# A three-part network over eight images: the first expert layer over sorted (token, expert) blocks, written out without a loop

## What is computed

```python
def _L0(x):                      # on the group-normalised image, 8 experts, hidden 384
    logits = x @ Wg + bg
    _, top_idx = top_k(logits, 2)
    gates = softmax(where(chosen, logits, -inf))
    y = gelu(x @ W1[e] + b1[e]) @ W2[e] + b2[e]          # for every expert e
    return sum_e y[e] * gates[e]
x = x + _L0(gn(x))               # 32 groups of 3 channels over all tokens
t = tokens(x)
t = t + causal_attention(ln(t))  # 6 heads of 16
t = t + _L1_ffn(ln(t))           # 4 experts, top 2 of softmax, hidden 384
```

## Time and profile before

| what | value |
|---|---|
| median of 3 runs | 1535.62 us (1528.77 to 1542.92) |
| profiled execution, span | 1533.6 us |
| instructions | 36404 |
| PE matmul busy | 1324.4 us, 86% |
| ACT busy | 934.1 us, 61% |
| DVE busy | 893.8 us, 58% |
| POOL busy | 716.0 us, 47% |
| DMA moved | 35.14 MB |

### The profile page before, as it was taken

How to read it: one execution, slowest core, us unless ns; L and a number is a source line. 1 busy time by engine, 2 the same in 40 slices (tenths; PEclk the granted TensorE clock), 3 DMA queues, 4 the chain that set the end, 5 groups by cost and what they waited for, 6 DMA issues and landing times.

```text
span 1533.6 us, 36404 instructions
## 1 busy us (share of the span) xinstructions
PE 1324.4 (86%) x12957; PEld 775.0 (51%) x12957; DVE 893.8 (58%) x2662; ACT 934.1 (61%) x1880; POOL 716.0 (47%) x656
## 2 busy tenths in 40 slices
PE   4778879888898899889898899888998898968978
PEld 1554543565536564466635565365644665333445
DVE  4865593388617784287724886177832866165362
ACT  2566537566675667656675667656676666703755
POOL 4765540467406572367605573075713665000355
PEclk9897998999999999899998999899999999956989
DMA  5000200300021000400004000210003000120100
GB/s 108 12 1 18 46 1 12 75 2 2 12 54 32 2 2 23 71 7 2 2 22 76 1 2 16 52 32 2 2 23 65 1 2 2 38 48 1 23 12 11
DMA packets 37424, 35.14 MB, mean 23 GB/s; under 512 B 26091, under 2 KB 28012, under 8 KB 37234
## 3 DMA queue, kind: packets, MB, share of 16 engines
q1 hardware_dynamic: 20594, 26.37, 8.8%
q10 hardware_dynamic: 16640, 6.29, 1.9%
HBM read 22.62 MB, written 9.63 MB: 21 GB/s over the span
## 4 chain that ended last, share of the span: by engine, by line
PE 30%; issue 26%; POOL 21%; DVE 13%; DMA 4%; ACT 2%; DVEq 1%; POOLq 1%; SPq 1%; ACTq 0%
POOL hidl L628 20%; PE ps_y L647 11%; PE ps_u L647 9%; PE ps_r L647 6%; DVE mpart L1156 4%; PE ps_m L647 3%; DVE xn L1138 1%; DMA ks<-qk_dram 1%; DMA qk_dram<-qk_l 1%; DVE acc L1104 1%; ACT hidh L934 1%; DVE yt L1288 1%; POOLq L608 1%; PE ps_m L666 1%; POOL rstd L609 1%
## 5 line engine op out<-in xcount | busy, mean ns | idle before, releaser
L628 POOL TENSOR_TENSOR hidl<-hid,hidh 128x512 f16<-128x512 f32 x576 | 670.7, 1185 | 686.2 <-ACT hidh L934 684.1
L933 ACT ACTIVATE hid<-ps_u 128x512 f32<-128x512 f32 x576 | 345.0, 599 | 391.8 <-PE ps_u L647 363.2
L1156 DVE TENSOR_REDUCE mpart<-ps_r 128x1 f32<-128x512 f32 (+2 forms) x576 | 297.3, 549 | 94.1 <-PE ps_r L647 79.8
L934 ACT ACTIVATE hidh<-ps_u 128x512 f16<-128x512 f32 x576 | 344.4, 598 | 0.0
L647 PEld LDWEIGHTS ps_y<-w2s,hidh 128*128 128x128 f16 x4608 | 276.4, 101 | 119.2 <-issue 24.1
L647 PE MATMUL ps_y<-w2s,hidh 128*128 128x96 f16 x4608 | 326.3, 210 | 8.0 <-DVE acc L1104 7.2
L647 PE MATMUL ps_r<-ks,qs 96*128 96x512 f16 (+2 forms) x576 | 199.9, 363 | 66.9 <-DVE mpart L1156 39.4
L647 PE MATMUL ps_y<-w2s,hidl 128*128 128x96 f16 x2304 | 231.0, 211 | 26.7 <-POOL hidl L628 26.6
L647 PE MATMUL ps_u<-xah,w1h 97*128 97x512 f16 x408 | 168.7, 414 | 29.8 <-ACT hidh L934 12.8
L965 ACT ACTIVATE probs<-ps_r 128x512 f32<-128x512 f32 (+3 forms) x352 | 152.9, 506 | 57.6 <-PE ps_r L647 57.2
L647 PE MATMUL ps_u<-xah,w1l 97*128 97x512 f16 x408 | 168.1, 412 | 0.0
(11 more groups left out here) (188 smaller groups left out, 1582.0 us busy)
## 6 DMA issues: line engine op xcount, KB each, us to landing
rb<-rsum_dram SPq DMA_DIRECT2D x24, 256.0 KB, 4.2
qs<-qk_dram SPq DMA_DIRECT2D x24, 192.0 KB, 4.9
ks<-qk_dram SPq DMA_DIRECT2D x24, 192.0 KB, 4.8
xin<-in_x_dram ACTq DMA_DIRECT2D x8, 384.0 KB, 4.1
qk_dram<-qk_h SPq DMA_DIRECT2D x16, 192.0 KB, 3.1
qk_dram<-qk_l SPq DMA_DIRECT2D x16, 192.0 KB, 3.5
out_dram<-xo ACTq DMA_DIRECT2D x8, 384.0 KB, 3.0
w_raw<-in_L_conv_W_dram SPq DMA_DIRECT2D x8, 288.0 KB, 5.1
```

The source lines that it names most:

```text
L628: g.tensor_tensor(hidl[:, grp.k % 2, j, :], hid[:, j, :], hidh[:, grp.k % 2, j, :], ALU.subtract).then_inc(hl_ready, 1)
L933: a.activation(hid[:, j, :], bank[:], ACT.Gelu, scale=1.0 / WS)
L934: a.activation(hidh[:, grp.k % 2, j, :], bank[:], ACT.Gelu, scale=1.0 / WS).then_inc(h_ready, 1)
L1156: v.tensor_reduce(mpart[:, h, i, part:part + 1], ps_r[k % 3][:, 0:w], AX, ALU.max).then_inc(mx_free, 1)
```

## The change

The first expert layer is computed only for the chosen pairs. Each image has 2048 (token, expert) pairs. They are sorted by expert, each expert's list is filled up to whole blocks of 128, and 23 blocks, a number fixed at build time, hold every possible split. The sorted order is made on the chip. DVE finds the two experts of each token; PE counts the earlier pairs of each expert by matmuls with a triangle of ones (`rank`); DVE turns counts into row numbers `slots` and the expert of each block `expert_of`. POOL scatters the rows of the image `xtok` into `xs_dram`, 16 indirect DMAs of 128 rows (`scatter`), SP loads all of it back (`xs_load`), and PE turns it and ACT and DVE split it (`xs_turn`, six quads: five of 4 blocks, one of 3).

The weights of a block's expert come by a DMA whose source is read from `expert_of` into a register of SP (`fetch`), 344 KB each, into a ring of 16 slots, `wring`. The first 16 blocks of an image are fetched in stage C before it (`prefetch`), the other seven when a quad is done (`refill`). The split weights are written to DRAM (`wq_dram`) once, at the start. A quad takes the place of a group: `first_layer` makes nine matmuls of 128 columns for each block in place of 512 columns for one expert, and the second layer has one matmul more a tile, which adds the bias. ACT copies the result out (`y_take`), SP stores it (`y_dram`), and POOL gathers it in token order, another 16 indirect DMAs (`gather`). DVE multiplies by the gates and adds (`merge`). Matmuls for the biases by the gates go away in both layers.

The stages are A, S, C in place of A, C, S, and C holds the q, k and value projections, 26 of the 72 maxima, the sums of the softmax and the sorting in of the next image; A holds the other 46 maxima; S holds routing, gather, merge, ln1 and scatter. `maxima` stands in slot 25 of the 28 of stage A, right before S. Image 1's iteration has its own table, with all 72 in slots 20 to 27 of stage A. The loop over images is written out: every iteration from -1 to 10 is unrolled. Image loads and stores move from ACT's queue to SP's. Layer normalisation is applied by two operations over half an image in place of one a tile.

```diff
+NBLK = (TOP * T + EA * (P - 1)) // P
+QUADS = [range(n, min(n + TC, NBLK)) for n in range(0, NBLK, TC)]
+GA, GC = len(QUADS), NC * EC
...
+def steps(it):
+
+
+    for n in range(GA + 1):
+        up = group_a(it, n) if n < GA else None
+        down = group_a(it, n - 1) if n else group_c(it - 3, GC - 1)
+        for j in range(TC):
+            yield Step("a", TC * n + j, up, down, j)
+    for n in range(STEPS + 2):
+        yield Step("s", n, None, None, n)
+    for n in range(GC):
+        up = group_c(it - 2, n)
+        down = group_c(it - 2, n - 1) if n else None
+        for j in range(TC):
+            yield Step("c", TC * n + j, up, down, j)
...
+NORM = [(15, "x_turn", 0, 1), (17, "x_turn", 1, 1), (18, "gn_stats", 0, 1), (20, "gn_mean", 0, 1),
+        (22, "gn_spread", 0, 1), (24, "gn_apply", 0, 1), (26, "logits_a", 0, 1), (27, "route_a", 0, 1)]
+ROUTE = [(0, "route_a", 1, 1), (0, "route_a", 2, 1), (2, "rank", 0, 1), (2, "exp_a", 0, 1)]
+IN_A = [(4, "store", 0, -3), (8, "x_load", 0, 1), (1, "ln2", 0, -2), (3, "ln2", 1, -2),
+        (5, "ln2_apply", 0, -2), (6, "ln2_apply", 1, -2), (9, "x2_turn", 0, -2), (11, "x2_turn", 1, -2),
+        (13, "logits_c", 0, -2), *maxima_at(0, 24, MAX_C, MAXU, -1), (25, "maxima", 0, -1), *NORM]
+IN_S = [(0, "exp_c", 0, -2), *ROUTE, (2, "gather", 0, 0), (2, "gather", 1, 0),
+        (5, "route_c", 0, -2), (6, "route_c", 1, -2), (7, "route_c", 2, -2), (8, "route_c", 3, -2),
+        (10, "merge", 0, 0), (11, "ln1", 0, 0), (11, "scatter", 0, 1), (11, "scatter", 1, 1), (13, "ln1_apply", 0, 0),
+        (16, "merge", 1, 0), (16, "gate_a", 0, 1), (17, "ln1", 1, 0), (17, "scatter", 2, 1), (17, "scatter", 3, 1),
+        (19, "ln1_apply", 1, 0), (21, "x1_turn", 0, 0), (24, "x1_turn", 1, 0)]
+IN_C = [(0, "sums", 0, -1), (1, "qk", 0, 0), (2, "xs_load", 0, 1), (3, "qk", 1, 0), (5, "qk", 2, 0), (7, "qk", 3, 0),
+        (8, "sum_inverse", 0, -1), (9, "val", 0, 0), (11, "val", 1, 0),
+        *maxima_at(15, TC * GC - 1, 0, MAX_C, 0), *fetches(range(12, 28, 2)),
+        (14, "normalise_y", 0, -1), (15, "normalise_y", 1, -1),
+        *sorted_in(range(13, 31, 3), 1), (27, "project", 0, -1), (30, "project", 1, -1)]
...
+            def fetch(b, blk):
+                s, _ = ring(b, blk)
+                e = sp.value_load(expert_of[0:1, b % 2, blk:blk + 1], min_val=0, max_val=EA - 1)
+                sp.dma_start(wring[:, s, :], wq_dram[bass.ds(e, 1)].rearrange("a p f -> p (a f)")
+                             ).then_inc(w_in[s], 16)
+
+            routed_end = 0
+
+            def prefetch(b, k):
+                if k == 0:
+                    sp.wait_ge(slots_ready, b + 1)
+                    if b:
+                        sp.wait_ge(y_full, routed_end)
+                for blk in range(2 * k, 2 * k + 2):
+                    fetch(b, blk)
+
+            def refill(group):
+
+                for blk in QUADS[group.n]:
+                    if blk + RING < NBLK:
+                        if blk == QUADS[group.n][0]:
+                            sp.wait_ge(y_full, grp.k)
+                        fetch(group.b, blk + RING)
...
+                if name == "xs_load":
+                    sp.wait_ge(scattered, 16 * TOP * TT * (b + 1))
+                    wait(sp, xs_ready, GA * b)
+                    if b > 1:
+                        sp.wait_ge(merged, NC * b)
+                    sp.dma_start(xs[:], xs_dram[b % 2].rearrange("(b q) c -> q b c", q=P)).then_inc(xs_in, 16)
...
+                if name == "gather":
+                    if k == 0:
+                        for i in range(YBUFS):
+                            pool.wait_ge(y_out[i], 16 * (GA // YBUFS) * (b + 1))
+                        pool.wait_ge(xs_ready, GA * max(b + 1, 2))
+                    for t in range(TC * k, TC * (k + 1)):
+                        for n in range(TOP):
+                            g.indirect_dma_start(
+                                out=ygot[:, n, t, :], out_offset=None, in_=y_dram[b % 2],
+                                in_offset=bass.IndirectOffsetOnAxis(ap=slots[:, b % 2, n, t:t + 1], axis=0)
+                            ).then_inc(gathered[k], 16)
+                if name == "scatter":
+                    if k == 0:
+                        pool.wait_ge(slots_ready, b + 1)
+                        pool.wait_ge(x_loaded, 16 * (b + 1))
+                        wait(pool, xs_in, 16 * (b - 1))
+                        if b < 2:
+                            pool.wait_ge(xs_zeroed, 32)
+                    for t in range(2 * k, 2 * k + 2):
+                        for n in range(TOP):
+                            g.indirect_dma_start(
+                                out=xs_dram[b % 2],
+                                out_offset=bass.IndirectOffsetOnAxis(ap=slots[:, b % 2, n, t:t + 1], axis=0),
+                                in_=xtok[:, b % XBUFS, t, :], in_offset=None).then_inc(scattered, 16)
...
+            def rank(b):
+
+                pe.wait_ge(mask_ready, b + 1)
+                shared()
+                mm(ps_m[:, 0:EA * (TT + 1)], before[:], maskb[:].rearrange("p t e -> p (t e)"), True, False)
+                for t in range(TT):
+                    last = mm(ps_m[:, EA * (t + 1):EA * (TT + 1)].rearrange("p (t e) -> p t e", e=EA), onesb[:],
+                              maskb[:, t:t + 1, :].to_broadcast([P, TT - t, EA]), False, t == TT - 1)
+                last.then_inc(m_full, 1)
+
...
+                    for i, blk in enumerate(QUADS[group.n]):
+                        s, use = ring(group.b, blk)
+                        if j == 0:
+                            pe.wait_ge(w_in[s], 16 * (use + 1))
+                        slot = slice(P * blk, P * (blk + 1))
+                        last = split(bank[:, P * i:P * (i + 1)], wring[0:ONE + 1, s, P * j:P * (j + 1)],
+                                     wring[0:ONE + 1, s, HID + P * j:HID + P * (j + 1)],
+                                     xsh[:, slot], xsl[:, slot], True)
...
+                mm(out, select[:], b2, True, False)
...
+            def y_take(group, seq):
+
+                k = group.b * GA + group.n
+                w = D * len(QUADS[group.n])
+                act.wait_ge(y_full, seq + 1)
+                wait(act, y_out[k % YBUFS], 16 * (k // YBUFS))
+                a.activation(ysort[:, k % YBUFS, :, :].rearrange("p b d -> p (b d)")[:, 0:w],
+                             ps_y[seq % 2][:, 0:w], ACT.Copy)
+                act.drain().then_inc(y_sorted, 1)
+                act.nop().then_inc(y_free[0], 1)
...
+                    blks = QUADS[k]
+                    w = P * len(blks)
+                    wait(act, xs_ready, GA * b + k - 1)
+                    shared()
+                    a.activation(xsf[:, k % 2, 0:w], ps_m[0:D, 0:w], ACT.Identity, bias=gshift[:], scale=grstd[:]
+                                 ).then_inc(xsf_ready, 1)
+                    a.activation(xsh[0:D, P * blks[0]:P * blks[0] + w], ps_m[0:D, 0:w], ACT.Identity,
+                                 bias=gshift[:], scale=grstd[:]).then_inc(m_free, 1)
...
+                if name == "merge":
+                    dve.wait_ge(gathered[k], 16 * PER_HALF * (b + 1))
+                    for n in range(TOP):
+                        v.tensor_tensor(ygot[:, n, tiles, :], ygot[:, n, tiles, :],
+                                        gate_a[:, n, tiles].unsqueeze(2).to_broadcast([P, TC, D]), ALU.mult)
+                    dve.drain()
+                    v.tensor_tensor(ygot[:, 0, tiles, :], ygot[:, 0, tiles, :], ygot[:, 1, tiles, :], ALU.add)
+                    dve.drain()
+                    v.tensor_tensor(xb[:, tiles, :], xb[:, tiles, :], ygot[:, 0, tiles, :], ALU.add
+                                    ).then_inc(merged, 1)
```

More of the change, by code:

```diff
@@ new lines, in maxima_at, with sorted_in, fetches @@
+def maxima_at(first, last, n0, n1, off):
+    return [(slot, "max", n0 + k, off) for slot, ks in spread(n1 - n0, range(first, last + 1)).items() for k in ks]
+MAX_C = 26
+def sorted_in(slots, off):
+    return [(slot, "xs_turn", q, off) for q, slot in enumerate(slots)]
+def fetches(slots):
+    return [(slot, "prefetch", n, 1) for n, slot in enumerate(slots)]
+NORM = [(15, "x_turn", 0, 1), (17, "x_turn", 1, 1), (18, "gn_stats", 0, 1), (20, "gn_mean", 0, 1),
+        (22, "gn_spread", 0, 1), (24, "gn_apply", 0, 1), (26, "logits_a", 0, 1), (27, "route_a", 0, 1)]
@@ L278, in run_chores, with chores @@
+def chores(table, it, step):
+    for name, unit, off in table[step.phase].get(step.slot, ()):
+        if off is None:
+            yield name, unit, 0
+        elif 0 <= it + off < NIMG:
+            yield name, unit, it + off
 def run_chores(m, chore, some):
@@ L521, in stack_qk @@
+                wait(sp, qk_out, 64 * b + 32 * (s + 1))
                 dst, parts = ((qs, (0, 1, 0)), (ks, (0, 0, 1)))[s]
@@ new lines, in _ @@
+            for it in range(-1, LAST_IT + 1):
+                table = schedule(it)
+                for s in steps(it):
```

(40 more changed lines are left out.)

1387 lines of the change are left out of this document (673 added, 714 removed).

## The result

The changed kernel takes 1608.4 us (median of 4 runs, 1607.9 to 1612.6) against 1536.5 for the kernel before, measured beside it: a ratio of 1.047, 95% interval 1.043 to 1.051. It is slower by 4.7%, where 1370 us was forecast. The profiled execution's span is 1610.8 us.

A forecast was written before the change was run, and what follows sets the result against it. No engine was full on average: PE and POOL together paced A and C, PE and ACT bound S. Start 293, six periods of 148 (888) and tail 187 gave 1368 us, so 1370; range 1240 to 1500.

The forecast's parts named there:

- Part 3: Stage S after the change: a chain on POOL of gathers, rstd and scatters sets its length, taken as 43 us.
- c: POOL's time for one indirect DMA of 128 rows, taken as 1.2 us; no row of the profile showed it.
- 13 + 24c: Length of S: 4 + 16c for gathers, 2, 8c for scatters, 2 and 5; 42 us, taken as 43.
- a rival at 15 in 100: In S, DVE and POOL shut each other out during descriptor writing: +15 us in S, 1470 us; 15 in 100.
- overhang: After S, C's first group waits for POOL's last scatters, about 8c less 5; taken as 5 us.
- The one rival that had the kernel slower than before, at 9 in 100: POOL's indirect DMAs in S and at the start decide: c = 2.3 gives 1635 us; 9 in 100.
- Part 5: Stage C after the change: PE 43 us, ACT 41, DVE 35, SP's queue level with the stage; taken as 50 (45 to 58).
- SP's queue decides: Rival: SP's queue or late weights (3 us a fetch) make PE wait for w_in; 1460 us, 8 in 100.
- Part 6: Outside the period: prologue 75 to 80 us, image 2's start at 293, six periods 888, tail 187; sum 1368 us.
- Parts 1, 2 and 4: PE's expert work 21.7 us for 55.5; stage A 43 us; maxima chain before S charged 4 + 3 us an image.

The follow-up runs named there:

- both faults out: Changed kernel with plain gathers and scatters on SP's queue, q and k first in C, sorted rows loaded at the end of S: 1403.7 us.
- v1: Against the version with gathers one a slot and scatters in C: scatters one at a time, eight in S and eight in C: 1512.7 us.

## Why the prediction was wrong

The forecast was 1368 us for the span, and it came to 1611: 104 us more at the start, 155 in the six full periods (1043 for 888; five near 179 and the last 150), 16 less in the tail (171 for 187).

**Part 3, stage S: the step that failed.** c was right: 1.25 from gather to gather for 1.2. What the sum 13 + 24c lacks is that the run of gathers stops the engines that S lives from. It took for granted that PE and ACT go on while POOL writes its lists of rows; only DVE against POOL was weighed, as a rival at 15 in 100, and its 15 us in S are the right size from the wrong cause. The measured price is 12 to 15 us an image beside the gathers. A second term was mis-sized: between the last gather and the first scatter the sum has 2 us, for rstd alone, and nothing for the merge, the statistics and the routing that DVE does before it. Measured are 14 us (826.5 to 840.5), a part of them because DVE too had stood in the stop until 829.3. Together S is 65 us for 43 and 5 of overhang. For every version with plain gathers it is 39 to 49. With the gathers spread S is 42.7, but that this is the 43 of the forecast is luck: that version has no scatters in S, and the 43 were the length of a chain with 16 of them. The one rival that had the kernel slower than before, at 9 in 100, asked for c of 1.9 or more; it named the right instructions and the wrong price.

**Part 5, stage C: the second.** 50 us forecast, bounds 45 to 58; measured 63. I set SP's queue "level with the stage" at 52 us and charged nothing for it. The length of the queue was beside the point. What counted is where in it `ks` stands: behind the load of the sorted rows and two writes, with a wait for each to land (their median is 5.1 us from issue to landing, and 2.3 where that load isn't ahead of them). PE's wait for it is 9.7 us. Taking it away gave back 4 to 5, which leaves most of the 13: with both faults out, 43 us of forecast work still take 59.4, a factor of 1.38 and not the 1.16 I took. How that splits into short waits and clock stays open. Rival "SP's queue decides" had the right engine and the wrong transfer: PE waited for `wring` 3.2 us in the whole span.

**Part 6, the start: the third.** Prologue 79.7 us, as forecast (75 to 80). After it nearly every step is late: A of image 1 starts at 161 for 128 (PE waits 17.7 us for the sorted rows) and lasts 116 us for 79. Its first groups stand behind the 16 gathers of image 0 (162.5 to 182.7), which are ahead of the subtractions in POOL's queue:

```profile
PE ps_y L677 <- POOL hidl L665: 23.4, 2, 19.4
```

S is then 56 for 48, C 64 for 38 (11.1 us for `ks`, and a clock of 0.55). I had summed this stretch from chores, with no queue at all. Late are A of image 0 and the gap by 33 us, A of image 1 by 37, S by 8 and C by 26: 104 us.

**Right.** Parts 1, 2 and 4: A with the chain is 50.7 us, forecast 50; PE's wait for the small DMA into `qs` is 3.7 us where it was looked at (A of image 1), forecast 4. The weights were no bound, the prologue and the tail came near. These were the parts that had rows of the trace of before to rest on. The range's upper end, 1500, was too low, since it took one late mechanism at a time, and three came together.

## What to carry to other kernels

Don't issue indirect DMAs of 128 rows back to back beside a tight exchange between PE and ACT: spread them, one to a step of the other engines' work, and look whether idle times without a releaser go. When steps are moved into another stage, write down the queue that issues their transfers in order, with each wait and landing, and the slot in which each result is wanted; a sum of the queue's length says nothing. A wait that is long in the profile is worth only what isn't right behind it: 9.7 us of wait here gave back 4 to 5.

## What the runs showed of the hardware that was not expected

- 16 indirect gathers at a pace of 1.25 us held up PE's signal to ACT by 3 to 8 us, two or three times an image; at 1.40 us about half as much in all; one a slot, 1.7 to 1.8 us apart in the mean, not. 32 plain DMAs of POOL (582 ns each, 0.53 us apart) didn't, and a run of eight indirect scatters cost 0 to 5.4 us.
- A drain behind an indirect gather takes 2.8 us, three times POOL's own 0.94.
- The load of the sorted rows, 2,944 rows of 384 bytes, goes with a late issue behind it on SP: the two writes of q took 4.71 us to issue there, those of k 0.89 later in the same stage; in v1, where a weight fetch stands behind that load, the fetch's issue took 3.3 us for 0.33.
